# Moving v's bias from TensorE to VectorE, and the residual's bias from VectorE to POOL, in an attention + mixture-of-experts kernel

## The reference

```python
x = _ln(x, ln1_w, ln1_b)
qk = _silu(x @ Wqk.T + bqk)
v = _silu(x @ Wv.T + bv)                       # width 512: the bias bv is part of the change
heads = qk[..., None, :] * gamma + beta        # four heads, then rope
attn = relu(einsum(quad_q, quad_k) / 64 + bias) ** 2
u = _silu(x @ Wg.T + bg) * (attn @ v + lin_q @ (lin_k.T @ v) / n)
out = _ln(u @ Wo.T + bo, ln2_w, ln2_b)         # ln2_b is the "second bias"
x = _layernorm(x_input + out)
x = _layernorm(x + moe(x))                     # shared expert + 8 routed experts, top 2
```

## Time and profile before

| | before |
|---|---|
| median of 3 runs | 923.8 us (920.94 to 925.58) |
| profiled execution | 921.3 us, span 919.5 us |
| mean granted clock | 0.995 |
| PE busy | 888.2 us |
| DVE busy | 685.0 us |
| ACT busy | 548.8 us |
| POOL busy | 264.2 us |

### The profile page before, as it was taken

One profiled execution on the slowest core, in us unless ns is written; L12 is line 12 of the kernel. 1 busy time (PEld: TensorE's weight loads), 2 busy tenths in 40 slices (PEclk: granted clock), 3 DMA queues, 4 the chain that ended last, 5 costly groups with the idle time before them and its releaser, 6 DMA issues.

```text
span 919.5 us, 17307 instructions
## 1 busy us (share of the span) xinstructions
PE 888.2 (97%) x5776; PEld 792.5 (86%) x5776; DVE 685.0 (74%) x1691; ACT 548.8 (60%) x1013; POOL 264.2 (29%) x188
## 2 busy tenths in 40 slices
PE   4999999999999898999999999999999999999995
PEld 3788788788778787999999999999999999999995
DVE  7699889889978599566566575766655579997476
ACT  5546656666636744556555455555555568887475
POOL 1000011001010047246635355452535345442000
PEclk9999999999999999999999999999999999999998
DMA  5142224223226424538656474855686648887723
GB/s 168 52 144 88 79 75 137 74 77 112 75 99 206 160 48 87 122 98 252 151 171 157 131 243 107 234 145 162 161 226 168 168 123 230 224 227 203 235 69 115
DMA packets 70167, 133.41 MB, mean 145 GB/s; under 512 B 14332, under 2 KB 55135, under 8 KB 62816
## 3 DMA queue, kind: packets, MB, share of 16 engines
q1 hardware_dynamic: 49904, 107.72, 35.7%
q0 software_dynamic: 16512, 21.32, 14.0%
q10 hardware_dynamic: 3696, 3.67, 1.2%
HBM read 98.18 MB, written 33.46 MB: 143 GB/s over the span
## 4 chain that ended last, share of the span: by engine, by line
PE 60%; DVE 5%; ACT 0%; issue 0%; DVEq 0%; ACTq 0%
PE bank L1718 26%; PE bank L1793 26%; PE bank L1738 3%; PE bank L1744 3%; PE bank L1778 2%; PE bank L1814 0%; DVE s_acc L1483 0%; DVE s_hl L1627 0%; PE bank L1715 0%; PE bank L1833 0%; DVE s_y L1467 0%; DVE s_until_map L1484 0%; DVE s_until_map L1485 0%; PE bank L1729 0%; DVE s_both L1374 0%
## 5 line engine op out<-in xcount | busy, mean ns | idle before, releaser
L1310 ACT ACTIVATE s_h<-bank,k_bfc 128x512 f32<-128x512 f32 (+1 forms) x216 | 134.5, 623 | 201.2 <-PE bank L1793 186.7
L1627 DVE TENSOR_TENSOR s_hl<-s_h,s_hh 128x512 fp32r<-128x512 f32 (+1 forms) x206 | 125.0, 607 | 139.8 <-ACT s_hh L1314 134.9
L1176 POOL DMA_INDIRECT residual_sums<-s_y,s_dest x64 | 108.7, 1699 | 182.2 <-DVE s_y L1557 168.5
L1314 ACT ACTIVATE s_hh<-s_h 128x512 fp32r<-128x512 f32 (+1 forms) x216 | 122.9, 569 | 9.1
L1793 PE MATMUL bank<-k_uh,s_wfc0h 128*128 128x512 f32 (+1 forms) x384 | 120.2, 361 | 0.0
L1718 PE MATMUL bank<-k_wpj1l,s_hh 128*128 128x256 f32 x384 | 108.9, 283 | 4.0 <-DVE s_hl L1627 4.0
L1718 PE MATMUL bank<-k_wpj1h,s_hl 128*128 128x256 f32 x384 | 108.2, 282 | 0.0
L1718 PE MATMUL bank<-k_wpj1h,s_hh 128*128 128x256 f32 x384 | 108.1, 282 | 0.0
L1718 PE MATMUL bank<-s_wpj0h,s_hh 128*128 128x256 f32 x344 | 96.6, 281 | 0.0
L1718 PE MATMUL bank<-s_wpj0h,s_hl 128*128 128x256 f32 x344 | 96.5, 280 | 0.0
L1718 PE MATMUL bank<-s_wpj0l,s_hh 128*128 128x256 f32 x344 | 96.5, 280 | 0.0
(11 more groups left out here) (348 smaller groups left out, 2246.5 us busy)
## 6 DMA issues: line engine op xcount, KB each, us to landing
k_wstage<-wall SPq DMA_DIRECT2D x42, 1024.0 KB
s_acc<-wall SPq DMA_DIRECT2D x14, 1024.0 KB
s_x_res<-x SPq DMA_DIRECT2D x8, 512.0 KB, 4.8
x_rows<-s_x SPq DMA_DIRECT2D x8, 512.0 KB, 3.4
residual_sums<-s_x SPq DMA_DIRECT2D x8, 512.0 KB, 4.3
x_parts<-s_x1h SPq DMA_DIRECT2D x8, 512.0 KB, 2.7
x_parts<-s_x1l SPq DMA_DIRECT2D x8, 512.0 KB, 3.7
k_uh<-x_parts SPq DMA_DIRECT2D x8, 512.0 KB
```

The source lines that it names most:

```text
L1176: pool.indirect_dma_start(RES, bass.IndirectOffsetOnAxis(dest[:, at:at + 1].bitcast(U32), 0), y[:, t, :], None, bounds_check=N + S - 1, co ...
L1310: nc.scalar.activation(h[j % 2][:, cols], b[:, cols], ACT.Gelu_apprx_tanh, bias=bfc[w][:, j:j + 1]).then_inc(h_ev, 1)
L1314: nc.scalar.activation(hh[j % RING][:, cols], h[j % 2][:, cols], ACT.Copy).then_inc(hh_rd, 1)
L1627: tt(hl[j % RING][:, cols], h[j % 2][:, cols], hh[j % RING][:, cols].bitcast(F32), ALU.subtract).then_inc(hl_rd, 1)
```

## The change

Three things. The matmul that lays v's bias into PSUM is gone, and with it the tile `bv2` and its making; the bias is loaded to all 128 partitions (`bv_all`), and DVE adds it while moving v from PSUM to SBUF, four operations behind the heads; ACT takes the silu in place, behind a new semaphore `v_biased`. ACT takes the logits copy ahead of this silu. The addition of residual and second bias goes from DVE to POOL, behind the o product of the same step; POOL's six pieces of the weight split follow it in steps 2 to 7.

```diff
-        bv2 = sb("bv2", [P, E], F32R)
+        bv_all = sb("bv_all", [P, E])
-            load(ld_c0, (raw_bv, a["rows"][:, 0, :]), (raw_bo[:, :], a["rows"][:, 1, 0:D]), (ones_raw[:, :], a["ones"]))
+            load(ld_c0, (bv_all[:, :], a["rows"][0:1, 0, :].to_broadcast([P, E])), (raw_bo[:, :], a["rows"][:, 1, 0:D]), (ones_raw[:, :], a["ones"]))
@@ POOL
-            pool.wait_ge(ld_s, 16)
-            for c in range(2):
+            def residual(b):
+                pool.wait_ge(ld_r, 16 * b)
+                pool.wait_ge(o_mm, 2 * b)
+                nc.gpsimd.tensor_tensor(x_res[:, :, :], x_res[:, :, :], ln2[:, 1:2, :].to_broadcast([P, TT, D]), ALU.add).then_inc(res_rd, 1)
+            def split(c, part):
                 w = (wfc1, wpj1)[c]
                 src = wstage[:, c, :].rearrange("p (k n) -> p k n", k=w[0].shape[1])
                 rows = w[0].shape[1] // 2
-                pool.wait_ge(o_mm, 4 + 6 * c)
-                nc.gpsimd.tensor_scalar(w[0][:, :, :], src, 1.0, 0.0, ALU.mult, ALU.add).then_inc(split_s, 1)
-                pool.wait_ge(split_s, 3 * c + 1)
-                for q in range(2):
-                    pool.wait_ge(o_mm, 4 + 6 * c + 2 * (q + 1))
-                    at = slice(q * rows, (q + 1) * rows)
+                if part == 0:
+                    nc.gpsimd.tensor_scalar(w[0][:, :, :], src, 1.0, 0.0, ALU.mult, ALU.add).then_inc(split_s, 1)
+                else:
+                    pool.wait_ge(split_s, 3 * c + 1)
+                    at = slice((part - 1) * rows, part * rows)
                     nc.gpsimd.tensor_tensor(w[1][:, at, :], src[:, at, :], w[0][:, at, :].bitcast(F32), ALU.subtract).then_inc(split_s, 1)
+            pool.wait_ge(ld_c, 16 * CONSTS)
+            for b in range(1, B + 1):
+                residual(b)
+                if b == 2:
+                    pool.wait_ge(ld_s, 16)
+                if 2 <= b < 8:
+                    split((b - 2) // 3, (b - 2) % 3)
@@ ACT
-                    for t in range(TT):
-                        act.wait_ge(v_mm, 4 * b + t + 1)
-                        nc.scalar.activation(v[:, t, :], bank[t][:, :], ACT.Silu).then_inc(v_ev, 1)
                 if not is_int(b) or b >= 3:
                     act.wait_ge(lg_mm, b - 2)
                     copy(logits[:, bass.ds((b - 3) * TT, TT), :], bank[7][:, :].rearrange("p (t n) -> p t n", t=TT)[:, :, 0:2 * NE]).then_inc(lg_ev, 1)
+                if main:
+                    for t in range(TT):
+                        act.wait_ge(v_biased, 4 * b + t + 1)
+                        nc.scalar.activation(v[:, t, :], v[:, t, :], ACT.Silu).then_inc(v_ev, 1)
@@ DVE
                     stt(heads[:, 0, :], qkr[:, 1, :], vec[:, GQ + 1:GQ + 2], heads[:, 0, :], ALU.mult, ALU.add).then_inc(heads_rd, 1)
+                if main:
+                    need(dve, u_mm, 4 * b)
+                    for t in range(TT):
+                        dve.wait_ge(v_mm, 4 * b + t + 1)
+                        tt(v[:, t, :], bank[t][:, :], bv_all[:, :], ALU.add).then_inc(v_biased, 1)
                 if o:
                     yo = [bank[6 + t // 2][:, t % 2 * D:t % 2 * D + D] for t in range(TT)]
-                    dve.wait_ge(ld_r, 16 * b)
-                    tt(x_res[:, :, :], x_res[:, :, :], ln2[:, 1:2, :].to_broadcast([P, TT, D]), ALU.add).then_inc(res_rd, 1)
                     stats(yo, TT, lambda t: t % 2 or dve.wait_ge(o_mm, 2 * (b - 1) + t // 2 + 1))
@@ DVE, ahead of step 0
-            bias_rows(bv2[0:BR, :], raw_bv)
@@ PE
-                        mm(bank[t][:, :], ones2[:, :], bv2[:, :], start=True, stop=False)
                         for k in range(KD):
                             last_i = three(bank[t][:, :], xTh[:, k, cols], xTl[:, k, cols], wv[0][:, k, :], wv[1][:, k, :],
-                                           False, k == KD - 1)
+                                           k == 0, k == KD - 1)
```

More of the change, by code:

```diff
@@ L242, in attention @@
         e_hh, e_hl = ([w[i][:, k, :] for i in range(2) for k in range(KD)] for w in (wg, wv))
-        raw_bv, raw_bo = raw[0:BR, 3584:3584 + E], shared["bpj_raw"][1 - SHW]
+        raw_bo = shared["bpj_raw"][1 - SHW]
         ld_v0, ld_c0, ld_c1, ld_c = sem("norm_consts_loaded"), sem("bias_rows_loaded"), sem("rope_loaded"), sem("consts_loaded")
@@ L263, in attention @@
         x1h_rd, x1l_rd, sh_st, x1_st = (sem(n) for n in ("x1h_ready", "x1l_ready", "parts_stored", "x1_stored"))
+        v_biased = sem("v_biased")
         tab_rd, zeroed = sem("tables_ready"), sem("bias_tiles_zeroed")
@@ L367, in _ @@
         def _(pool):
-            for tile in (bv2, bo2, *bpj):
+            for tile in (bo2, *bpj):
                 nc.gpsimd.memset(tile[:, :].bitcast(F32), 0.0).then_inc(zeroed, 1)
@@ L678, in _ @@
             nc.vector.tensor_copy(ones2[:, :], ones_raw[:, :])
-            dve.wait_ge(zeroed, 4)
-            bias_rows(bv2[0:BR, :], raw_bv)
+            dve.wait_ge(zeroed, 3)
             weights_lo(2)
@@ L724, in fc @@
                     pe.wait_ge(split_s, 6)
-                    pe.wait_ge(tab_rd, 5)
+                    pe.wait_ge(tab_rd, 4)
                 need(pe, h_ev, j - 1)
@@ L768, in step @@
                         pe.wait_ge(wl_rd, 2)
-                        pe.wait_ge(tab_rd, 2)
+                        pe.wait_ge(tab_rd, 1)
                     for t in range(TT):
@@ L786, in step @@
                         pe.wait_ge(wl_rd, 4)
-                        pe.wait_ge(tab_rd, 3)
+                        pe.wait_ge(tab_rd, 2)
                     pe.wait_ge(ul_rd, 4 * b)
```

## The result

| | before | after |
|---|---|---|
| median of 4 runs | 923.3 us | 937.6 us (936.54 to 938.98) |
| ratio, 95% interval | | 1.0159 (1.0142 to 1.0176) |
| profiled execution | 921.3 us, span 919.5 | 938.98 us, span 936.9 |
| PE / DVE / ACT / POOL busy | 888.2 / 685.0 / 548.8 / 264.2 us | 887.0 / 695.5 / 548.8 / 282.8 us |

The starts of the steps (first q/k matmul) say where the time went. Step 7 is read to the start of the last logits matmuls behind it.

A forecast was written before the change was run, and what follows sets the result against it. PE was taken as the bound, with an equally long chain over DVE (0.16 us spare). Terms 5.9 + 1.0 + 4.0 + 1.8 + 1.5 + 0.3 = +14.5 us gave 938 us, range 930 to 946.

The forecast's parts named there:

- The bound: Loop step: PE bounds, but the chain over o, POOL, DVE and att is as long, with 0.16 us spare.
- Every steady step: Steps 2 to 6: POOL's later end less spare time, 1.33 us each in 3, 4, 6 and 0.9 in 2, 5.
- (c): Rival, steps 1 to 7: PE stays the bound, 6.5 us saved in full, 923 us; chance 0.08.
- (d): Rival: as (c), and step 0's gate is held less than thought, 916 us; chance 0.05.
- Part 1: PE: bias matmuls go, 0.93 us saved per step, 7.4 in eight steps; larger bias load taken as zero.
- Part 2: DVE: four bias additions of 0.68 us, 2.72 per step; residual addition of 1.22 leaves; net +1.5 per step.
- Part 3: ACT's order: logits copy ahead of v's silu costs nothing; silu, x1, xn and lq come some 7 us later.
- Part 4: POOL: residual addition taken as 2.4 us, POOL ends 1.5 us later in the step and DVE's moments stand until then.
- (b): Rival: POOL also holds DVE's bias addition, moments 1.0 us later, six steps +6 us, 944 us; chance 0.11.
- Step 0: Gate waits for v's silu behind the heads, starts 4.2 us later, plus 1.7 for a fallen clock: +5.9 us.
- Steps 1, 7 and 8: Step 1 +1.0 us from DVE's net work, step 7 +1.5 without spare time, step 8 +0.3 from POOL's addition.
- The sum: Whole kernel: +14.5 us, on the median of 923.8 us giving 938.3, rounded to 938; forecast's chance 0.62.

The follow-up runs named there:

- e3: Changed kernel with ACT's scaling of x1 and xn put ahead of v's silu: 936.6 us, ratio 1.0161 to before.
- e11: Changed kernel with POOL's addition of residual and bias made twice in every step: 962.7 us in one run.
- e4: Changed kernel with POOL's addition released by the heads instead of the end of o: 929.1 us, ratio 1.0077 to before.
- e10: Changed kernel, v's bias first in step 0, POOL's addition at the heads, weight piece behind u's low parts, silu behind x1, xn after step 0: 920.0 us.
- e7: Kernel before with the 32 bias matmuls of v left out and v's bias not added: 915.6 us, ratio 0.992.
- e1: Changed kernel with the addition of residual and bias back on DVE, ahead of the statistics of o: 935.9 us, ratio 1.0146 to before.
- e6: Changed kernel with ACT's logits copy put back behind v's silu: 966.2 us in one run.
- e9: Changed kernel with x1 and xn scaled ahead of v's silu and POOL's addition at the heads, weight piece left behind o: 929.6 us in one run.

## Why the prediction was right, point by point

*The bound.* The reading that PE's chain and the one over o, POOL, DVE and att were equal to 0.16 us held. Every steady step moved by what POOL's end moved less that spare time: forecast 1.33 and 0.9, measured 1.4 and 0.9. e3 moved what stands ahead of POOL's end, and the step stayed but for 0.15 us; e11 moved POOL's end, and the step followed; e4 took POOL's end out of the way, and x1 decided. Rivals (c) and (d) needed steps of 32.6 us; these came only when the holds were gone (e10), not in the changed kernel.

*Part 1.* 0.93 us per step: e7 shows 0.92 in the loop. The larger load made ACT wait 1.43 us for the output weights in place of 0.48, without effect.

*Part 2.* The additions cost 2.48 us for four, not 2.72, since they overlap a little; the statistics ended at 167.55. Neither is on the path, so this was without effect.

*Part 3.* ACT was where it was expected: x1 at 17.0 us of the step against 17.9 forecast, 1.6 us before POOL's end at 18.7. It decided only in e4, where POOL was out of the way.

*Part 4.* POOL's addition took 2.38 us against 2.4. The Trainium skill's statement (SBUF — State Buffer, "Who interferes with whom") that an instruction of DVE with at most one SBUF input is not held beside GpSimd, if it is outside the 2-port performance modes, is now shown by e4 for a tensor_tensor from PSUM and SBUF; that one with two is held, by L141, by L143 in e3 and by the residual addition in e1. The prediction left that condition out, and it says that no row shows an operation with one SBUF input beside POOL. The trace of before has such operations, in the experts' stage, and two of them, a cast and a tensor_scalar, stand until POOL ends. The second:

```profile
337.91 1.29 POOL L1208 TENSOR_TENSOR s_hl<-s_h,s_hh 128x512 fp32r<-128x512 f32 x1 [1.52 <-ACT s_hh L1314]
338.06 1.17 DVE L1442 TENSOR_SCALAR s_from_small<-s_n_big 128x8 f32<-128x8 f32 x1
```

So (b) was argued away too broadly: it is false for the bias additions, which are tensor_tensor operations from PSUM and SBUF, but a cast here and tensor_scalar operations here and in e11 were held with one SBUF input. Whether the 2-port modes are the reason no run here shows.

*Step 0, the term with the largest miss*: 5.9 forecast, 6.8 measured. The gate came at 29.30 (forecast 29.15). But PE ended v at about 23.1, a microsecond sooner than I took from the trace of before, so that the idle time was 6.2 us, not 5.1; and the slow stretch lasted 5.0 us at 0.50, not the 3.4 of the earlier trace rows. The gate took 8.1 us instead of 5.6, a price of 2.5 us where I had put 1.7, inside the bounds that I gave. This price varies from execution to execution. Six experiments also have v's bias behind the heads in step 0 (e1, e3, e4, e6, e9, e11); in all seven traces the gate comes at 29.2 to 29.3, but step 0 takes 34.8 to 35.8 us, and the granted clock from 29.3 to 34.3 goes with it: 0.50 in the three longest, 0.58 and 0.59 at 35.2, 0.68 and 0.69 at 34.8. e6 is the changed kernel word for word up to step 2 and took 34.8, or +5.8: within this spread neither the forecast nor the miss of 0.9 us says much.

*Steps 1, 7 and 8.* +0.9 against +1.0; +1.4 against +1.5; what is behind step 7 adds another 0.4 to the logits matmuls of the last step, against 0.3.

*The sum.* +14.5 forecast, +15.4 in the attention's trace, +14.3 between the medians. That 938 and 937.6 agree so closely is luck: step 0 alone varies by a microsecond between traces, and the experts' stage by one to two.

## What to carry to other kernels

When a trace shows a tiny operation that takes long, look for who ends at the same moment on POOL: the price belongs to the pairing, not to the operation, and moving either engine's work moves it to the next operation with two SBUF inputs (e1, e3). Put POOL's work that reads SBUF beside DVE operations that were seen to run free there: here the bias additions (PSUM and one SBUF tile) and the statistics (one input), but not tensor_scalar or a cast from SBUF to SBUF (e11, and the trace before). With the same work, placing alone was worth 8.5 us here (e4). And check the first step of a pipeline by itself: an order that is harmless in the loop cost 6.4 us in step 0, because there PE had nothing else to do, and a stall long enough to lower the clock is paid again behind it.

## What the runs showed of the hardware that I had not expected

- A held DVE queue lets small operations through between two POOL operations: in e3 L142 ran between POOL's addition and its piece, and only L143 was held again. The changed kernel does the same in its step 7, where L141 takes 0.97 us, L142 0.15 and L143 2.37.
- An operation with one SBUF input can be held: tensor_scalar in e11 for 2.31 us, and a cast (1.19 us) and a tensor_scalar (1.17 us) in the trace before. The same L144 and the same cast take 0.17 us where they are not held.
- The granted clock after idle time of PE: 1.92 us, no fall (1.00); 3.50 us, 0.77 over the next 7.4 us; 3.88 us, 0.68 over 5.4; 6.19 us, 0.50 over 5.0. The length of the idle time alone does not say how much is lost: in step 0 of e4 it was 4.82 us and the clock 0.50 over the next 5.0, in e6 it was 5.59 us and the clock 0.69. The 1.5 us waits of the changed kernel's loop cost no clock (1.00 in every step from 1 to 7). The two experiments with waits of 3.9 and 4.7 us in every loop step (e11, e6) came out 11 and 5 us above expectation.
